# A graph layer's 65-column fp32 products rewritten as 32-column products in four quarters of TensorE's array

## The reference, cut to what matters

```python
def _L3_gnn_ref(feat, src, dst, W, attn_l, attn_r):   # feat: (3125, 256), HEADS = 4, OUT_DIM = 64
    ft = (feat @ W.T).reshape(n, HEADS, OUT_DIM)
    a1 = jnp.einsum('nhd,hd->nh', ft, attn_l)
    a2 = jnp.einsum('nhd,hd->nh', ft, attn_r)
    e = jax.nn.leaky_relu(a1[src] + a2[dst], negative_slope=0.2)
    m = jax.ops.segment_max(e, dst, num_segments=n)
    ex = jnp.exp(e - m[dst])
    s = jax.ops.segment_sum(ex, dst, num_segments=n)
    a = ex / s[dst]
    out = jax.ops.segment_sum(ft[src] * a[:, :, None], dst, num_segments=n)
    return jax.nn.elu(out.reshape(n, HEADS * OUT_DIM))
...
    h = jnp.maximum(_layernorm(x, axis=-1), 0.0)
    x = x + _L3_gnn_ref(h, src, dst, L3_gnn_W, L3_gnn_attn_l, L3_gnn_attn_r)
```

## Time and profile before

| | |
|---|---|
| Median of 3 runs | 2154.23 us (2144.46, 2154.23, 2157.07) |
| The profiled execution, its own time | 2139.71 us |
| Its span in the trace | 2137.8 us |
| Mean granted TensorE clock over the span | 0.914 |
| TensorE busy with matmuls | 1862.9 us, 87% of the span |
| VectorE busy | 1305.1 us, 61% |
| Layer 3's last block (from line 2119 on) | from 1578 us to the end, 559.8 us |

### The profile page before, as it was taken

The page is one execution under the profiler, slowest core; times in us unless marked ns, Lnnn a source line. Parts: engine busy times, 40 slices in busy tenths (PEclk is TensorE's granted clock), DMA queues, the critical chain, the costliest instruction groups (busy, mean ns, idle before and its releaser), DMA issues. The chain is left out here.

```text
span 2137.8 us, 22846 instructions
## 1 busy us (share of the span) xinstructions
PE 1862.9 (87%) x7207; PEld 1136.3 (53%) x7207; DVE 1305.1 (61%) x1926; ACT 507.0 (24%) x738; POOL 1078.9 (50%) x1646
## 2 busy tenths in 40 slices
PE   3868967789979888988766999999889999999996
PEld 1246742266656555656554756778753444434443
DVE  5976758845524343443423565665587788878887
ACT  0500020034543434434333534200240000000000
POOL 3888888888888888888888700000032000000000
PEclk8955569899999999999888999999899999999998
DMA  9788850015544534443423432487223333434432
GB/s 352 316 323 338 323 187 23 9 36 182 185 138 140 167 110 156 151 155 135 143 93 139 155 114 81 147 300 227 93 48 91 89 81 86 102 89 106 96 83 69
DMA packets 335681, 313.04 MB, mean 146 GB/s; under 512 B 274432, under 2 KB 320234, under 8 KB 325867
## 3 DMA queue, kind: packets, MB, share of 16 engines
q1 hardware_dynamic: 220153, 265.90, 36.8%
q10 hardware_dynamic: 89654, 45.29, 7.2%
q0 software_dynamic: 25792, 0.88, 1.0%
HBM read 180.44 MB, written 131.55 MB: 146 GB/s over the span
## 5 line engine op out<-in xcount | busy, mean ns | idle before, releaser
L409 POOL DMA_INDIRECT table<-valT,idxT x806 | 777.5, 965 | 174.7 <-issue 139.9
L2234 PE MATMUL psum<-wgt,big 128*65 128x384 f32 (+4 forms) x1600 | 530.7, 493 | 8.6 <-DVE wgt L2185 8.5
L2185 DVE SCALAR_TENSOR_TENSOR wgt<-ratio,l3q,fcj 128x768 f32<-128x768 f32 (+4 forms) x442 | 408.0, 947 | 90.1 <-PE psum L2234 84.1
L2234 PEld LDWEIGHTS psum<-wgt,big 128*65 128x65 f32 x1600 | 219.4, 138 | 310.6 <-issue 283.9
L905 PE MATMUL psum<-hx,region 128*128 128x257 f32 x1250 | 303.9, 388 | 35.8 <-issue 28.5
L905 PE MATMUL psum<-region,g 128*128 128x512 f32 (+1 forms) x672 | 282.5, 566 | 1.5 <-DVE big L683 1.5
L905 PEld LDWEIGHTS psum<-hx,region 128*128 128x128 f32 x1250 | 229.7, 193 | 77.7 <-issue 39.5
L683 DVE TENSOR_TENSOR big<-big,psum 128x512 f32<-128x512 f32 (+1 forms) x325 | 209.5, 664 | 96.3 <-PE psum L905 65.4
L407 POOL MEMSET rest<- 128x256 f32 x805 | 264.4, 328 | 1.1 <-DMA table<-valT,idxT 0.6
L905 PEld LDWEIGHTS psum<-region,g 128*128 128x128 f32 x672 | 124.5, 195 | 126.7 <-issue 109.8
L1153 POOL PARTITION_ALL_REDUCE edges<-edge x1 | 0.5, 515 | 351.9 <-DVEq L1530 351.9
(11 more groups left out here) (250 smaller groups left out, 1656.6 us busy)
## 6 DMA issues: line engine op xcount, KB each, us to landing
table<-tk SPq DMA_DIRECT2D x25, 3200.0 KB
tk<-table SPq DMA_DIRECT2D x25, 1664.0 KB
tk<-table SPq DMA_DIRECT2D x25, 1536.0 KB
fcj<-counts_b SPq DMA_DIRECT2D x125, 192.0 KB, 2.6
counts_t<-region ACTq DMA_DIRECT2D x25, 800.0 KB
counts_b<-region ACTq DMA_DIRECT2D x25, 800.0 KB
table<-valT,idxT POOLq DMA_INDIRECT x806
l2m<-counts_b SPq DMA_DIRECT2D x20, 640.0 KB, 5.4
```

Of the source, the lines that this page charges most:

```text
L409: eng.indirect_dma_start(out=table, out_offset=bass.IndirectOffsetOnAxis(idxT[:, c:c + 1], 0), in_=valT[:, c, :], in_offset=None).then_inc ...
L2185: eng.scalar_tensor_tensor(out=wgt[:, n % NW, u, 0:w], in0=rb[:, 2 * i + u, t0 * P:t0 * P + w], scalar=qs[:, k, 2 * i + u:2 * i + u + 1], ...
L2234: last = eng.matmul(acc[p % 2][u][0:FW, b, 0:hi - lo], ftx[:, k, 2 * i + u, :], wgt[:, n % NW, u, lo:hi], start=k == 0, stop=k == NT - 1, ...
```

## The change

The product of 65 columns (64 features and the ones) is split. The 64 features of a head become two products of 32 columns each (product): for one piece of a range, the four products of two heads and two halves write to partitions 0, 32, 64 and 96 of the same PSUM bank. The denominators are products of their own (total): the stationary operand is e2 of the head, one column repeated 32 times, and the four products of two heads and two pieces write to partitions 0 to 31, 32 to 63, 64 to 95 and 96 to 127 of a third bank. So e2 is no longer carried in the ones column, and the scaling of the features covers 64 columns instead of 65. The pieces are cut at a tile's edge (512 and 384 columns, 384 and 384, 384 and 309). wgt has 4 buffers instead of 3. VectorE and TensorE now wait for both heads of a step together. ScalarE copies the features of both heads at once for each piece, and the denominators (dT); TensorE turns full blocks of 128. The sums take three banks for each of the two sets, and the ratio rows move to banks 6 and 7, so the wait for them before pass 1 goes.

```diff
--- before.py
+++ after.py
@@ -2024,7 +2024,7 @@
     with ExitStack() as ctx:
         def buf(name, shape, dt=F32):
             return sb(name, shape, dt, ctx)
-        NW, NC, FIRST = 3, 4, 3
+        NW, NC, FIRST = 4, 4, 3
         MOST = RANGES[0][1]
         UPPER = [p for p, (i, r) in enumerate(PASSES) if i]
         qs, e2, ng = buf("l3q", [P, NT, H]), buf("l3e2", [P, NT, H]), buf("l3ng", [P, H])
@@ -2032,15 +2032,18 @@
         rb = buf("ratio", [P, H, NP])
         wgt = buf("wgt", [P, NW, 2, MOST * P])
         cj = buf("fcj", [P, NC, MOST, P], BF16)
-        oT = buf("oT", [P, 2, MOST * P])
+        oT, dT = buf("oT", [P, MOST * P]), buf("dT", [P, 4 * P])
         den, rden = buf("fden", [P, 2, MOST]), buf("frden", [P, 2, MOST])
         neg = buf("fneg", [P, MOST, D])
         o = hx[:, :, 0:D]
-        acc = [[psum[:, 4 * b + 2 * u:4 * b + 2 * u + 2, :] for u in range(2)] for b in range(2)]
-        pR = psum[:, 4:6, :]
+        flat = lambda t: t.rearrange("p b n -> p (b n)")
+        acc = [psum[:, 3 * b:3 * b + 2, :] for b in range(2)]
+        sums = [psum[:, 3 * b + 2, :] for b in range(2)]
+        scores_at = [flat(psum[:, 2 * u:2 * u + 2, :]) for u in range(2)]
+        pR = psum[:, 6:8, :]
         width = lambda r: min(N, (RANGES[r][0] + RANGES[r][1]) * P) - RANGES[r][0] * P
-        half = lambda r: -(-width(r) // 2)
-        pieces = lambda r: [(0, width(r))] if width(r) <= 512 else [(0, half(r)), (half(r), width(r))]
+        half = lambda r: (RANGES[r][1] + 1) // 2
+        pieces = lambda r: [(0, width(r))] if width(r) <= 512 else [(0, half(r) * P), (half(r) * P, width(r))]
         span = lambda r: slice(RANGES[r][0], RANGES[r][0] + RANGES[r][1])
         ROWS_AT, TURN_AT, DIVIDE_AT, FINISH_AT, STORE_AT = 6, 3, 6, 10, 16
         WIDE_AT = (17, 20)
@@ -2082,7 +2085,7 @@
         def _(eng):
             eng.wait_ge(s_("exp"), 2)
             for k in range(FIRST, NT):
-                eng.tensor_tensor(ftx[:, k, :, :], ftx[:, k, :, :], e2[:, k, :].unsqueeze(2).to_broadcast([P, H, FW]), ALU.mult)\
+                eng.tensor_tensor(ftx[:, k, :, 0:HD], ftx[:, k, :, 0:HD], e2[:, k, :].unsqueeze(2).to_broadcast([P, H, HD]), ALU.mult)\
                    .then_inc(s_("ft"), 1)
 
         @block.scalar
@@ -2092,7 +2095,7 @@
             eng.activation(e2[:, :, :], rr[:, :, 0:H], ACT.Exp, scale=0.2).then_inc(s_("exp"), 1)
             nt = RANGES[0][1]
             for u in range(2):
-                eng.activation(rb[:, u, 0:nt * P], acc[0][u].rearrange("p b n -> p (b n)")[:, 0:nt * P], ACT.Exp,
+                eng.activation(rb[:, u, 0:nt * P], scores_at[u][:, 0:nt * P], ACT.Exp,
                                bias=ng[:, u:u + 1], scale=-0.8).then_inc(s_("rbp"), 1)
             eng.activation(rr[:, :, H:2 * H], rr[:, :, H:2 * H], ACT.Exp, scale=-0.8).then_inc(s_("exp"), 1)
             for g in range(7):
@@ -2100,14 +2103,13 @@
                 eng.wait_ge(s_("rowed"), g + 1)
                 eng.activation(rsb[:, 4 * g * P:4 * g * P + w], pR[0:H, g % 2, 0:w], ACT.Copy).then_inc(s_("rows"), 1)
             for p, (i, r) in enumerate(PASSES):
-                nb = len(pieces(r))
                 n = pieces(r)[0][1]
                 eng.wait_ge(s_("m"), 2 * NT * (p + 1))
                 if p:
                     eng.wait_ge(s_("turned"), p)
-                for u in range(2):
-                    last = eng.activation(oT[0:FW, u, 0:nb * n].rearrange("p (b n) -> p b n", b=nb), acc[p % 2][u][0:FW, 0:nb, 0:n], ACT.Copy)
-                    last.then_inc(s_("oT"), 1)
+                for bank, (lo, hi) in enumerate(pieces(r)):
+                    eng.activation(oT[:, lo:hi], acc[p % 2][:, bank, 0:hi - lo], ACT.Copy).then_inc(s_("oT"), 1)
+                eng.activation(dT[:, 0:n], sums[p % 2][:, 0:n], ACT.Copy).then_inc(s_("dT"), 1)
                 if i:
                     eng.wait_ge(s_("neg"), UPPER.index(p) + 1)
                     eng.activation(neg[:, 0:RANGES[r][1], :], neg[:, 0:RANGES[r][1], :], ACT.Exp).then_inc(s_("elu"), 1)
@@ -2134,19 +2136,22 @@
                 short = t0 + nt == NT
                 whole = nt - 1 if short else nt
                 eng.wait_ge(s_("turned"), p + 1)
-                sums = [acc[p % 2][u][:, 0, 0:nt * FW].rearrange("p (t f) -> p t f", f=FW) for u in range(2)]
+                first = -(-pieces(r)[0][1] // P)
+                feats = flat(acc[p % 2])[:, 0:nt * P].rearrange("p (t u f) -> p t u f", u=2, f=HD)
+                totals = sums[p % 2].rearrange("p (t u b c) -> p b u t c", u=2, b=2, c=P // 4)
                 parts = [(P, 0, whole)] + ([(N - (NT - 1) * P, whole, nt)] if short else [])
-                for u in range(2):
+                for bank in range(len(pieces(r))):
                     for q, lo, hi in parts:
-                        ch.do(eng.tensor_scalar(den[0:q, u, lo:hi], sums[u][0:q, lo:hi, HD], 1e-37, None, ALU.max))
+                        lo, hi = max(lo, bank * first), min(hi, bank * first + first)
+                        if lo < hi:
+                            ch.do(eng.tensor_scalar(den[0:q, :, lo:hi], totals[0:q, bank, :, lo - bank * first:hi - bank * first, 0], 1e-37, None, ALU.max))
                 ch.after()
                 for q, lo, hi in parts:
                     ch.do(eng.reciprocal(rden[0:q, :, lo:hi], den[0:q, :, lo:hi]))
                 ch.after()
-                for u in range(2):
-                    for q, lo, hi in parts:
-                        ch.do(eng.tensor_tensor(o[0:q, t0 + lo:t0 + hi, HD * (2 * i + u):HD * (2 * i + u + 1)], sums[u][0:q, lo:hi, 0:HD],
-                                                rden[0:q, u, lo:hi].unsqueeze(2).to_broadcast([q, hi - lo, HD]), ALU.mult))
+                for q, lo, hi in parts:
+                    ch.do(eng.tensor_tensor(o[0:q, t0 + lo:t0 + hi, 2 * HD * i:2 * HD * i + 2 * HD].rearrange("p t (u f) -> p t u f", u=2), feats[0:q, lo:hi, :, :],
+                                            rden[0:q, :, lo:hi].rearrange("p u t -> p t u").unsqueeze(3).to_broadcast([q, hi - lo, 2, HD]), ALU.mult))
                 ch.after()
                 eng.sem_inc(s_("ev"), 1)
                 if i:
@@ -2181,7 +2186,7 @@
                         if n == 0:
                             eng.wait_ge(s_("rbp"), u + 1)
                         if n >= NW:
-                            eng.wait_ge(s_("m"), 2 * (n - NW) + u + 1)
+                            eng.wait_ge(s_("m"), 2 * (n - NW) + 2)
                         eng.scalar_tensor_tensor(out=wgt[:, n % NW, u, 0:w], in0=rb[:, 2 * i + u, t0 * P:t0 * P + w],
                                                  scalar=qs[:, k, 2 * i + u:2 * i + u + 1],
                                                  in1=here.rearrange("p k d -> p (k d)")[:, 0:w],
@@ -2207,15 +2212,35 @@
             def turn(p):
                 r = PASSES[p][1]
                 t0, nt = RANGES[r]
-                eng.wait_ge(s_("oT"), 2 * p + 2)
-                for u in range(2):
-                    for t in range(nt):
-                        q = min(P, N - (t0 + t) * P)
-                        last = eng.transpose(acc[p % 2][u][0:q, 0, t * FW:(t + 1) * FW], oT[0:FW, u, t * P:t * P + q], ident[0:FW, 0:FW])
+                r = PASSES[p][1]
+                eng.wait_ge(s_("oT"), sum(len(pieces(PASSES[e][1])) for e in range(p + 1)))
+                for t in range(nt):
+                    q = min(P, N - (t0 + t) * P)
+                    eng.transpose(flat(acc[p % 2])[0:q, t * P:(t + 1) * P], oT[:, t * P:t * P + q], ident[:, :])
+                eng.wait_ge(s_("dT"), p + 1)
+                n = pieces(r)[0][1]
+                for lo in range(0, n, P):
+                    last = eng.transpose(sums[p % 2][0:min(P, n - lo), lo:lo + P], dT[:, lo:min(n, lo + P)], ident[:, :])
                 last.then_inc(s_("turned"), 1)
+
+            def product(p, k):
+                i, r = PASSES[p]
+                for bank, (lo, hi) in enumerate(pieces(r)):
+                    for u, v in ((0, 0), (0, 1), (1, 0), (1, 1)):
+                        at = HD * u + P // 4 * v
+                        eng.matmul(acc[p % 2][at:at + P // 4, bank, 0:hi - lo], ftx[:, k, 2 * i + u, P // 4 * v:P // 4 * v + P // 4],
+                                   wgt[:, (NT * p + k) % NW, u, lo:hi], start=k == 0, stop=k == NT - 1, skip_group_check=True)
+
+            def total(p, steps):
+                i, r = PASSES[p]
+                for k in steps:
+                    for u in range(2):
+                        for bank, (lo, hi) in enumerate(pieces(r)):
+                            at = P // 4 * (2 * u + bank)
+                            last = eng.matmul(sums[p % 2][at:at + P // 4, 0:hi - lo], e2[:, k, 2 * i + u:2 * i + u + 1].to_broadcast([P, P // 4]),
+                                              wgt[:, (NT * p + k) % NW, u, lo:hi], start=k == 0, stop=k == NT - 1, skip_group_check=True)
+                last.then_inc(s_("m"), 2 * len(steps))
```

(11 more changed lines are left out.)

## The result

The changed kernel takes 2050.8 us (median of 4 runs, 2048.7 to 2052.1), the kernel before 2149.4 in the runs beside it: a ratio of 0.954, 95% interval 0.950 to 0.958. I had forecast 2416 us, slower, with a chance of 0.50. What came is the outcome of the rival "four abreast", which had 0.34, and 23 us under its 2074; the forecast's range reached down to 2050 for that rival alone.

A forecast was written before the change was run, and what follows sets the result against it. The prediction took TensorE to bound layer 3. Products +258.4, start +1.2 and transposes +2 summed to +262 us: 2402 on the profiled execution's 2139.7, 2416 on the median 2154.2; 8-in-10 range 2050 to 2450 us.

The forecast's parts named there:

- four abreast: Rival, chance 0.34: layer 3's products fill all four quarters together, six-tile TensorE step 1.94 us, VectorE the bound, 2074 us.
- The bound: Layer 3, 559.8 of 2137.8 us, is bound by TensorE; VectorE, with 451.93 us of work, would be next.
- The unit: Time of one layer 3 matmul, whatever its output width: 0.3225 us for 384 columns, 0.4293 for 512.
- if TensorE starts matmuls in order: Layer 3 products each overlap a neighbour by half: 12 units a six-tile step, +258.4 us in all, chance 0.50.
- bounds of 6 and 24 units: Products of a six-tile step: 1.94 us if four run at once, 7.74 us if none overlap.
- 262 us of cost: Whole change in layer 3: products 258.4 us, start 1.2 us, transposes 2 us, all added time.
- Its VectorE step: VectorE's six-tile step in the four abreast rival: 2 x 1.017 us and 0.04 for starting, 2.07 us, the bound.
- Weight loads: TensorE's loads for 32-column products: hidden at no cost; four abreast, 24 x 0.062 = 1.49 us, under 1.94.
- The new wait at the start: TensorE waits for both heads of wgt in the first step, one VectorE instruction more: about 1.2 us.
- Turning: TensorE's transposes between passes: six plus three take 1.0 us instead of 0.74; +2 us over the passes.
- Buffers and waits: VectorE's wait for both heads' products, with four buffers, and pass 1's wait for the ratio rows: nothing.
- The narrow passes: In the four abreast rival, two denominators fill two quarters, so narrow steps keep 4 units, 1.29 us.

The follow-up runs named there:

- the run in one quarter: Changed kernel with all feature products from a pass's second step on sent to quarter 0, denominators unchanged: 141.4 us a pass, 2986 us (one run).
- the run with four in a row: Changed kernel with feature products reordered so both pieces of a quarter come in a row, four matmuls to one quarter: 49.3 us a pass, ratio 0.956.
- the run with hardly any denominators: Changed kernel with the denominators' products only in the first step of each pass: median 2038.4 us against 2059.9 for the changed kernel beside it.
- the two runs above: Changed kernel with three wgt buffers: ratio 0.956. Kernel before with four wgt buffers, pieces cut at a tile's edge and joint waits, products still 65 columns: ratio 1.002.
- six and twelve in a row: Changed kernel with a quarter's features and denominators in a row, six matmuls: 69.8 us a pass, ratio 1.029; two steps together, twelve: 130.3 us, 2668 us.

## Why the prediction was wrong

**The bound** was read rightly: TensorE alone, and VectorE next.

**The unit** held: 0.3225 us for 384 columns and 0.4293 for 512 (a seven-tile step of 2 x (0.4293 + 0.3225 + 0.4293) = 2.36 us; the stretch of 59.0 us holds 22 of them and 3 of the six-tile steps, 52.0 + 5.8, and 1.1 of transposes, 58.9 in sum). That fewer columns of output are worth nothing by themselves was shown by the run in one quarter.

**The step that failed** is "if TensorE starts matmuls in order": the second matmul of product 1 would hold up the first of product 2. It does not. The trace of before could not show it, since all its products started at the same column of the array and so shared their quarters with the one ahead; an order seen there told nothing of separate quarters. I had bounds of 6 and 24 units and took 12 for want of a row with overtaking, though that lack spoke as little for the one as for the other. Measured: 6 units for a six-tile step, as long as no more than four matmuls in a row fall to one quarter. So the 262 us of cost, 258.4 of them for the products, turned into 94.6 of gain.

The Trainium skill, "TensorE: Matmul & The Clock Gate", section "Part 3: Packing small matmuls", has matmuls start and end strictly in program order; the starts in the seven-tile pass and the run with four in a row contradict it for quarters. For the ends the rows agree with the page as far as a matmul's signal goes: it came only after the end of longer matmuls ahead in the program (last section).

**The rival "four abreast"** had the mechanism and, at 2074, was 23 us too high. Its VectorE step was mis-sized: I took 2 x 1.017 + 0.04 = 2.07 us from mean durations. But VectorE's instructions overlap at their ends, like the matmuls. In the run with hardly any denominators 27 of them, of 1.014 us each, take 25.18 us in a row, 0.93 each:

```profile
1720.12 25.18 DVE L2190 SCALAR_TENSOR_TENSOR wgt<-ratio,l3q,fcj 128x768 f32<-128x768 f32 x27 [0.21 <-PE psum L2231]
```

A pass there takes 47.6 us; less about 1.6 for the division, that is 1.84 a step. So TensorE, at 1.94, stayed the bound of the first pair's passes by a hair.

**Weight loads** at nothing: right, 24 in a step under 1.94 us. **The new wait at the start**, 1.2 us: it is there, 1.1 us of the 2.23 for the first two instructions of wgt. **Turning**: 0.80 and 0.33 us for six plus three transposes, 1.13 where I had 1.0, and the group behind them takes 1.43 us instead of 1.29:

```profile
1709.68 0.80 PE psum L2219 x6
1710.48 0.33 PE psum L2223 x3
1710.81 1.43 PE psum L2231 x16
```

These 0.14 us are as many as a change between halves and quarters cost; that they have the same cause was not tested. **Buffers and waits** at nothing: right, by the two runs above. The narrow passes keep four units, as the rival said; at 36.3 and 26.4 us they are a little longer than the 34.7 and 25.7 of before.

## What to carry to other kernels

If a stationary operand has no more than 32 columns, or can be cut into such pieces, and TensorE is the bound, four float32 products side by side cost here the time of one. Count then by units in the fullest quarter, and spread the products so that no more than four matmuls in a row (two float32 products) fall to one quarter. With pieces of unequal length one signal on a step's last matmul stayed enough here. Keep one width throughout: each change between halves and quarters cost 0.14 us here. Take an engine's step from distances in a stretch where it is the bound, not from the mean duration of an instruction, and after a large gain look again at what was split for the old bound.

## What I had not expected of the hardware

Matmuls in different quarters start out of program order, each quarter with four places; a fifth stops the issue for all: 6, 8.5 and 16 units a step with four, six and twelve in a row fit this and no other number of places. In the seven-tile pass the program's last matmul of a step, 384 columns of denominators, carries the signal that the step is done, and it starts before the last 512-column ones of other quarters. Whether the signal waits for those can be read where ScalarE waits for a pass's last one. First the end of a seven-tile pass, where the last matmuls of 384 columns start at 1652.68:

```profile
1652.68 0.90 PE L2240 MATMUL psum<-wgt,l3e 128*32 128x384 f32 x4
1653.40 0.61 PE L2240 MATMUL psum<-wgt,l3e 128*32 128x512 f32 x2
1654.08 0.98 ACT L2111 ACTIVATE oT<-psum 128x512 f32<-128x512 f32 x2 [30.60 <-PE psum L2240]
```

Then the end of a six-tile one, where all have the same length:

```profile
1703.04 0.83 PE L2240 MATMUL psum<-wgt,l3e 128*32 128x384 f32 x8
1703.94 0.87 ACT L2111 ACTIVATE oT<-psum 128x384 f32<-128x384 f32 x2 [48.39 <-PE psum L2240]
```

ScalarE starts 0.07 us after the last end on TensorE in both: 1653.40 + 0.61 = 1654.01 and 1703.04 + 0.83 = 1703.87. A matmul of 384 columns lasts 0.50 us in these rows, so the one that carries the signal ended near 1653.2, 0.9 us before ScalarE moved. Starts go out of order here, but the signal of a matmul came only when those ahead of it in the program had ended. The second seven-tile pass shows the same 0.07 us. The ends of matmuls in a trace are modelled; the equal distance in both cases is what this rests on.
